# One of a step's 72 columns of samples fetched by plain DMAs from register addresses, issued by SyncE and ScalarE

## The reference

```
x = x + L0(gn(x))   3x3 convolution, then 64x64
x = x + L1(gn(x))   deformable 3x3 convolution, two groups of 32 channels
x = x + L2(gn(x))   focal modulation: depthwise 3x3, 5x5, 7x7 with gelu, gates, modulator
x = x + L3(gn(x))   triangle product of two sigmoid gates, a third gate
```

## Time and profile before

| | |
|---|---|
| median of 3 runs | 12371.41 us (12371.2 to 12372.86) |
| the profiled execution: time, span | 12375.1 us, 12373.3 us |
| granted TensorE clock, mean | 0.773 |
| busy: PE, DVE, ACT, POOL | 7826.9, 5178.4, 1654.1, 8754.7 us |
| DMA | 101 GB/s on average |

### The profile page before, as it was taken

How to read it: one execution, slowest core, us unless ns; L and a number is a source line. 1 busy time by engine, 2 the same in 40 slices (tenths; PEclk the granted TensorE clock), 3 DMA queues, 4 the chain that set the end, 5 groups by cost and what they waited for, 6 DMA issues and landing times.

```text
span 12373.3 us, 133594 instructions
## 1 busy us (share of the span) xinstructions
PE 7826.9 (63%) x46178; PEld 6378.0 (52%) x46178; DVE 5178.4 (42%) x6138; ACT 1654.1 (13%) x2837; POOL 8754.7 (71%) x9269
## 2 busy tenths in 40 slices
PE   5766667666467765554457775655457776655488
PEld 3554455545457644444447654444446664444474
DVE  3344444443344444343344444343344444344333
ACT  1011111110011112110001111210001111211015
POOL 3777777777777777777777777777777777777700
PEclk8887778877678877776678877777678887877689
DMA  2333334333244422432234422332224432343271
GB/s 86 102 88 97 111 89 111 105 94 102 73 125 160 130 66 78 115 95 61 67 102 146 167 68 71 100 110 71 57 80 146 171 93 64 92 112 91 62 248 56
DMA packets 878254, 1255.70 MB, mean 101 GB/s; under 512 B 183384, under 2 KB 663320, under 8 KB 860248
## 3 DMA queue, kind: packets, MB, share of 16 engines
q0 software_dynamic: 294912, 604.57, 19.2%
q1 hardware_dynamic: 512216, 601.04, 14.4%
q10 hardware_dynamic: 70912, 47.20, 1.2%
HBM read 1069.49 MB, written 245.50 MB: 106 GB/s over the span
## 4 chain that ended last, share of the span: by engine, by line
POOL 68%; issue 23%; PE 4%; DVE 1%; DMA 1%; ACT 0%; POOLq 0%; PEld 0%; SPq 0%; PEldq 0%; ACTq 0%; DVEq 0%
POOL gathered L471 68%; PE stage L1033 2%; PE stage L926 1%; DVE srow L1561 0%; DMA gathered<-table,idx 0%; PE acc L926 0%; DVE gathered L1554 0%; PE pt L926 0%; POOLq L469 0%; PE wtb L926 0%; PE acc L1175 0%; PEld acc L1175 0%; PE stage L988 0%; POOLq L467 0%; POOLq L477 0%
## 5 line engine op out<-in xcount | busy, mean ns | idle before, releaser
L471 POOL DMA_INDIRECT gathered<-table,idx x9216 | 8730.2, 947 | 2979.2 <-issue 2801.6
L1175 PE MATMUL acc<-stt,room 128*128 128x128 f32 (+1 forms) x30600 | 4372.0, 308 | 234.6 <-ACT stt L901 234.6
L1175 PEld LDWEIGHTS acc<-stt,room 128*128 128x128 f32 (+1 forms) x30600 | 4220.1, 221 | 543.5 <-ACT stt L901 341.5
L1164 PE MATMUL pt<-mat,srow 128*128 128x128 f32 x2048 | 507.2, 394 | 3682.6 <-DVE srow L1561 3682.2
L1164 PEld LDWEIGHTS pt<-mat,srow 128*128 128x128 f32 x2048 | 327.5, 196 | 3882.9 <-DVE srow L1561 3870.6
L1530 DVE COPY idx<-idxn 128x18 uint32<-128x18 uint32 x512 | 98.1, 192 | 5195.8 <-DMA gathered<-table,idx 5187.5
L1561 DVE TENSOR_REDUCE srow<-gathered 128x576 f32<-128x2304 f32 x512 | 2081.1, 4065 | 0.1
L1554 DVE TENSOR_TENSOR gathered<-gathered,wtb 128x2304 f32<-128x2304 f32 x512 | 1306.1, 2551 | 63.0 <-DMA gathered<-table,idx 62.6
L901 ACT ACTIVATE stt<-pt 128x512 f32<-128x512 f32 x512 | 305.9, 597 | 5968.0 <-PE pt L1164 5965.6
L926 PE MATMUL stage<-room,mat 128*128 128x512 f32 (+1 forms) x1360 | 791.4, 712 | 296.6 <-DVE room L1425 70.8
L1033 PE MATMUL stage<-room 128*128 128x128 f32 x7680 | 890.2, 278 | 12.8 <-DMA room<-toep 10.6
(11 more groups left out here) (206 smaller groups left out, 3931.7 us busy)
## 6 DMA issues: line engine op xcount, KB each, us to landing
gathered<-table,idx POOLq DMA_INDIRECT x9216
room<-toep SPq DMA_DIRECT2D x64, 1792.0 KB, 19.0
room<-toep SPq DMA_DIRECT2D x64, 1280.0 KB, 11.5
room<-toep SPq DMA_DIRECT2D x64, 768.0 KB
table<-room SPq DMA_DIRECT2D x64, 512.0 KB, 2.9
toep<-in_taps SPq DMA_DIRECT2D x128, 224.0 KB
toep<-in_taps SPq DMA_DIRECT2D x128, 160.0 KB
room<-in_x SPq DMA_DIRECT2D x4, 4096.0 KB
```

Source lines behind the costliest of these rows:

```text
L471: nc.gpsimd.indirect_dma_start(gat[r][:, k % K9 * G + k // K9, :], None, table[b].rearrange("(n e) -> n e", e=PAIR), bass.IndirectOffsetOn ...
L1164: ins = nc.tensor.transpose(pt[:, m, :], srow[r % 2][:, m * P:(m + 1) * P], M["ident"])
L1175: ins = nc.tensor.matmul(acc[a][:, 0:W], wk[0:kk, m, dx, block_at * C:block_at * C + P], stt[s][0:kk, m, dx:dx + W], start=start and m == ...
```

## The change

POOL leaves out the last column (`AT_K` = 17) of row 0 (`AT_R`) in every step but the first. For this column DVE writes the next step's addresses, the index times 64, into `column` (inside `indices`, behind L1525). At time 1 of step n, SP stores that column of 128 addresses to `column_d` in DRAM, waits until it has landed, and waits until row 0 of step n is summed. It then loads eight addresses from DRAM into registers and issues eight plain DMAs of 512 bytes, one per pixel, each from the address in a register; it does so eight times in the step, two blocks for each row, for pixels 0 to 63. ScalarE does the same for pixels 64 to 127: at time 1 it waits for `column_out` and for `summed`, and its blocks stand at 3r + 1 and 3r + 1.5, ahead of its copy L901 of the row. DVE waits for `pixels_in` ahead of row 0 of step n + 1. Two semaphores (`folded`, `moved`) go; `next_image` drains DVE instead.

```diff
+AT_R, AT_K = 0, GK - 1
+CHUNK = 8
...
+        column_d = nc.dram_tensor("column_d", [STEPS, P], I32).ap()
...
 # POOL
                     for r in range(ROWS):
                         v = n * ROWS + r
+                        own = GK if r != AT_R or isinstance(n, int) else AT_K
...
-                        for k in range(GK):
+                        for k in range(own):
...
 # SP
+                def fetch_column(n):
+                    sp.wait_ge(column_given, n)
+                    sp.dma_start(column_d[ds(n, 1), :].rearrange("o p -> p o"), column[:]).then_inc(column_out, 16)
+                    sp.wait_ge(column_out, 16 * n)
+                    sp.sem_inc(started, 1)
...
+                        if k == 0:
+                            fetch_column(n + 1)
+                            sp.wait_ge(summed, n * ROWS + AT_R + 1 + ROWS)
+                            sp.sem_inc(started, 1)
+                        per = P // CHUNK // 2 // ROWS
+                        for q in range(per * k, per * (k + 1)):
+                            yield 3 * k + 1 + 3 * (q % per) / per
+                            fetch_pixels(n + 1, nb, q)
...
 # ACT
+                def fetch_pixels(n, b, q):
+
+                    act.load(regs, column_d[ds(n, 1), CHUNK * q:CHUNK * (q + 1)])
+                    for j in range(CHUNK):
+                        at = act.snap(regs[j], min_val=0, max_val=(NPAIR - 2) * PAIR)
+                        act.dma_start(pixel(CHUNK * q + j), table[b][ds(at, ENTRY)].unsqueeze(0)).then_inc(pixels_in, 16)
...
                     for r in range(ROWS):
+                        yield 3 * r + 1
+                        if r == 0 and not last:
+                            act.wait_ge(column_out, 16 * n + 16)
+                            act.wait_ge(summed, n * ROWS + AT_R + 1 + ROWS)
+                            act.sem_inc(started, 1)
+                        per = P // CHUNK // 2 // ROWS
+                        for q in range(per * r, per * (r + 1) if not last else 0):
+                            yield 3 * r + 1 + (q % per) / per
+                            fetch_pixels(n + 1, nb, P // CHUNK // 2 + q)
                         yield 3 * r + 2
...
 # DVE
+                    if not (isinstance(n, int) and n == 0):
+                        if not (isinstance(n, int) and n == 1):
+                            dve.wait_ge(column_out, 16 * n - 16)
+                        ts(column[:], idxn[:, AT_R, AT_K:AT_K + 1], float(PAIR), None, ALU.mult).then_inc(column_given, 1)
...
-                    dve.wait_ge(landed[r], 16 * GK * (n + 1))
+                    dve.wait_ge(landed[r], 16 * GK + 16 * (AT_K if r == AT_R else GK) * n)
+                    if r == AT_R and not (isinstance(n, int) and n == 0):
+                        dve.wait_ge(pixels_in, 16 * P * n)
```

More of the change, by code:

```diff
@@ L242, in build @@
         idx = sb("idx", [P, ROWS, GK], U32)
+        column = sb("column", [P, 1], I32)
         wtn = sb("wtn", [P, ROWS, GK, 4])
@@ L371, in build @@
         table_out = sems("table_out0", "table_out1")
-        off_in, off_used, chain, idx_given, wt_given, moved, started = sems(
-            "off_in", "off_used", "chain", "idx_given", "wt_given", "moved", "started")
+        off_in, off_used, chain, idx_given, wt_given, started = sems(
+            "off_in", "off_used", "chain", "idx_given", "wt_given", "started")
+        column_given, column_out, pixels_in = sems("column_given", "column_out", "pixels_in")
         landed = sems(*(f"landed{r}" for r in range(ROWS)))
@@ L439, in planes, with pixel @@
             return d[b].rearrange("c (h r) w -> r c h w", r=2)[par, :, ds(4 * t, 4), :]
+        def pixel(p):
+            return gat[AT_R][p:p + 1, AT_K % K9 * G + AT_K // K9, :]
         def half(a, par, n=C):
@@ L474, in step @@
                                 .then_inc(landed[r], 16)
+                step(0, 0)
                 for b in range(NB):
-                    with pool.Fori(b * PER, (b + 1) * PER) as n:
+                    with pool.Fori(max(b * PER, 1), (b + 1) * PER) as n:
                         step(n, b)
@@ L671, in start @@
                     load_offsets(0, 0, 0)
+                regs = [sp.alloc_register(f"at{j}") for j in range(CHUNK)]
+                def fetch_column(n):
[4 more added lines that the diff above has]
+                def fetch_pixels(n, b, q):
+                    sp.load(regs, column_d[ds(n, 1), CHUNK * q:CHUNK * (q + 1)])
+                    for j in range(CHUNK):
+                        at = sp.snap(regs[j], min_val=0, max_val=(NPAIR - 2) * PAIR)
+                        sp.dma_start(pixel(CHUNK * q + j), table[b][ds(at, ENTRY)].unsqueeze(0)).then_inc(pixels_in, 16)
                 def step(n, b, i):
@@ L687, in step @@
                         sp.dma_start(x2[:, 2 * STEPS * W:(2 * STEPS + 1) * W], xs[:, 0, :]).then_inc(x2_out, 16)
-                    if b == 0:
-                        for k in range(ROWS):
-                            yield 3 * k + 1
+                    last = isinstance(n, int) and n == STEPS - 1
+                    for k in range(ROWS):
+                        yield 3 * k + 1
+                        if b == 0:
                             bands(ROWS * i + k)
+                        if last:
+                            continue
+                        if k == 0:
[6 more added lines that the diff above has]
+                            fetch_pixels(n + 1, nb, q)
                 meet = meeting(sp)
@@ L892, in close, with fetch_pixels @@
                         act.dma_start(out[:, ds(n(u) * TILE, TILE)], res[u]).then_inc(res_out[u], 16)
+                regs = [act.alloc_register(f"at{j}") for j in range(CHUNK)]
+                def fetch_pixels(n, b, q):
+                    act.load(regs, column_d[ds(n, 1), CHUNK * q:CHUNK * (q + 1)])
+                    for j in range(CHUNK):
+                        at = act.snap(regs[j], min_val=0, max_val=(NPAIR - 2) * PAIR)
+                        act.dma_start(pixel(CHUNK * q + j), table[b][ds(at, ENTRY)].unsqueeze(0)).then_inc(pixels_in, 16)
                 def step(n, b, i):
+                    last = isinstance(n, int) and n == STEPS - 1
+                    nb = b + 1 if isinstance(i, int) and i == PER - 1 else b
                     for r in range(ROWS):
+                        yield 3 * r + 1
[7 more added lines that the diff above has]
+                            fetch_pixels(n + 1, nb, P // CHUNK // 2 + q)
                         yield 3 * r + 2
@@ L1357, in context_fold @@
                     scale(S["wq"], M["wq"])
-                    scale(gws[:], gw[:]).then_inc(folded, 1)
+                    scale(gws[:], gw[:])
                     yield 13
@@ L1362, in context_fold @@
                     tt(b_q2, PB[2][:, 1:2], V["b_q"], ALU.add)
[L1363 removed]
+                    tt(b_gate2[0:8, :], PB[2][0:8, 2:3], b_gate, ALU.add)
                 def operands_fold(b, i):
                     yield 11
[L1367 removed]
+                    scale(S["ccen"], M["ccen"])
                     yield 13
                     dve.wait_ge(shift_p, 2 * b + 2)
[L1370 removed]
+                    nc.vector.tensor_copy(b_cen, PB[2][:, 0:1])
                 def context(b, i):
@@ L1565, in next_image @@
                 def next_image(b):
-                    nc.vector.tensor_copy(base[:], base0[:]).then_inc(moved, 1)
-                    dve.wait_ge(moved, b + 1)
+                    nc.vector.tensor_copy(base[:], base0[:])
+                    dve.drain()
                 def start():
```

5 lines of the change are left out of this document (1 added, 4 removed).

## The result

| | before | after |
|---|---|---|
| median | 12372.01 us (4 runs beside the changed kernel's) | 13202.49 us (13182.17 to 13212.49, 4 runs) |
| ratio | | 1.0669, 95% interval 1.0655 to 1.0683: slower |
| span of the profiled execution | 12373.3 us | 13208.0 us |
| gathers on POOL | 9216 | 9089 |

The direction was as forecast, the size was not: +830 us where +273 was the forecast, and above the end of the range, 12950. (On some chips the kernel before itself took 18367 to 18585 us in place of 12375; what ran there stands in one table under group 3 and is compared with nothing else.)

A forecast was written before the change was run, and what follows sets the result against it. POOL's gather queue was taken to bound the kernel. Three images losing 118 (depthwise) + 26 (modulate) make 432 us, less 159 saved: +273 on 12375.1, 12648, set at 12645 for the median; range 12205 to 12950.

The forecast's parts named there:

- POOL bounds the kernel before; 127 gathers are worth 159 us: POOL's gather queue never stands still, 1.252 us per gather; leaving out one in 127 steps saves 159 us.
- SP's eight blocks fit, DVE's operation and the wait in SP's step cost nothing: SP idles most of a step, so 41 us of blocks fit; DVE's 0.2 us and SP's first wait cost nothing.
- ScalarE's blocks stand in the chain and turn the gain into a loss: ScalarE runs in order; most blocks delay copies TensorE's products need, losing 432 us in three images against 159 gained.
- A block costs c = 5.1 us: One load of eight registers, 1.65 us, plus eight DMA issues at 0.43, 3.4 us; bounds 2.2 and 18.4.
- A depthwise step is 90.5 + 4c: From g, the last gelu's end, to the same place next step: 110.9 us against 88.9, 22 lost per step.
- Modulate is 54.5 + 8c: Step length in the stage behind depthwise, all eight blocks in the way: 95.3 us, 26 us lost over four steps.
- Operands, close and table steps: Steps of 46 to 53 + 8c, 87 to 94 us, losing few us that light steps (without background) take up.
- free lag: POOL needs row 0's sum only three rows later, so 58 us of lateness cost nothing and light steps win them back.
- Rival 1: The chain keeps up and POOL stays full: 12212 us; needs a depthwise step under 96 us; chance 0.22.
- Rival 2: The block is cheap, about 2.4 to 3.1 us; at 2.4 a depthwise step is 100.1, total 12308; chance 0.10.
- Rival 3: A block's load costs several trips to DRAM: 12933 us at c = 6.6, 14000 above 8; 0.10 with rival 4.
- Rival 4: The pixels come late for DVE at next step's row 0; decides only with c near 8; 0.10 with rival 3.

The follow-up runs named there:

- group 3: Runs with one register load per block or with pixels split 96 to 32, and repeats of other runs, on chips where the kernel before took 18366.87 to 18584.81 us.
- e1: Changed kernel with nobody fetching the left-out column: no address store, no blocks on SyncE or ScalarE; 12215.75 us, ratio 0.9871 to the kernel before.
- e2: Changed kernel with ScalarE's 64 pixels left out, SyncE storing the addresses and fetching its 64; 12217.13 us, ratio 0.9872 to the kernel before.
- e3: Changed kernel with SyncE's 64 pixels left out, SyncE only storing the addresses and ScalarE fetching its 64; 13090.23 us, ratio 1.0578 to the kernel before.
- e5b: Changed kernel with ScalarE's waits kept and its blocks taken out; 12220.06 us, ratio 0.9875 to the kernel before.
- e7b: Changed kernel with ScalarE's register loads taken out and its 64 DMAs kept, from fixed addresses; 12438.22 us, ratio 1.0049 to the kernel before.
- e4: Changed kernel with ScalarE's two blocks of a row, and the waits ahead, moved behind the row's second copy; 12992.84 us, ratio 1.0499 to the kernel before.
- e8b: Changed kernel with all 128 pixels fetched by SyncE in sixteen one-load blocks, none by ScalarE; 13841.36 us, ratio 1.1185 to the kernel before.
- e10b: Changed kernel with column_d as one fixed row, so one register load per block, not two; 20301.12 us, against 18366.87 before on the same chip.

## Why the prediction was wrong in size

By its own steps:

- **POOL bounds the kernel before; 127 gathers are worth 159 us.** Right: 158.4 (e1).
- **SP's eight blocks fit, DVE's operation and the wait in SP's step cost nothing.** Right by themselves: 1.4 us (e2). Beside ScalarE's blocks SyncE's cost 112 us (e3), most of them in image 0, and why stays open.
- **ScalarE's blocks stand in the chain and turn the gain into a loss.** Right, and shown: with them 13090 to 13202, without them 12217 to 12220.
- **A block costs c = 5.1 us.** The issues were 0.40, not 0.43: 3.2 us in place of 3.4. The load was said to be "one trip to DRAM", 1.65 us. It is two loads of 1.10 us and their register work, 2.4. So c = 5.7, and this term was mis-sized. The nearest row for the price of one load was a fair guide (1.10 for 1.65); that the source line stands for two was not seen, and no row of the kernel before could show it. By the prediction's own formula c = 5.75 gives 8 x 24.6 - 58 = 139 and 4 x 11.6 = 46 per image, 3 x 185 - 159 = +396. This explains 123 of the 557 us that are missing.
- The two prices that were quoted beside it from the Trainium skill: "Runtime: NRT & Kernel Launch", "Instruction fetch mechanics", 200 ns per register even in bulk; the rows give 1.10 us for eight, 0.14 each, and the same 1.10 for one, so by the trace it is a price per load and not per register. "DMA: Bandwidth & Descriptors", "Latency and other measured facts", 600 ns as the floor; the minimum in the trace is 0.99 (a pointer's load on SyncE), and no load came near 0.6.
- **A depthwise step is 90.5 + 4c.** The slope is about right: 4.7 and 4.2 between the kernels above. The fixed part is 93 (e5b) in place of 90.5, and the blocks under the bands add some four: 16.4 us from the gelus' end to the copy's (4144.88 to 4161.29) where 2c + 0.6 is 12.1; and a table load of 1.28 us shows behind the wait. 118 against 113.5 by the formula: 8 x 4.5 x 3 = 108 us. The blocks of row 0 begin at g + 35 (first pixel at g + 37), where 33 was the forecast, but not for its reason. SP stores the column when `indices` are done, at g + 24 and not at g + 18, and the blocks begin 10.5 us after that. A landing of 6.5 us or more belongs to any step; 2.0 were assumed, the quickest landing of a small DMA in the earlier trace rows. At most 4 of the 10.5 can be the bands' doing. (Whether the column would pass the bands on another queue was not tried. In the trace of the kernel before, a store of ScalarE's, issued on its own queue at 3828.76, landed at 3850.44, and the last band at 3850.02: that one did not pass them.)
- **Modulate is 54.5 + 8c.** 100.5 at c = 5.75, measured 99: right.
- **Operands, close and table steps lose "few us that the light steps beside them take up".** This is the step that failed: a term put at nothing. Operands are 103 us by measurement, 92 to 99 by 46 to 53 + 8c; triangle 102, and no formula was written for it; close 92. (4 x 13.7 + 2 x 13.4 + 4 x 3.4) = 95 us per image, 286 in three. And image 0 loses 75 us, where nothing was set down. The trace has the blocks in the way of the background's own operations too: in an operands step ScalarE idles on its own queue 24 us ahead of L959 and 41 ahead of L878 and L889, in all 65, where the kernel before has 0.2. The argument "the light steps take it up" is wrong in itself. A light step returns lag, so that the chain is early again (those without background take 74 us, not the 88.9 of the forecast); it does not return time in which POOL stood still. The 58 us of free lag are spent once, in the depthwise stage, and modulate, operands, triangle and close follow with only one light step between them (the norm, 83 us).
- **Together:** 123 (c) + 108 (depthwise) - 18 (modulate) + 286 + 75 = 574, against the missing 557. The terms are not exact (step lengths are means, and the free lag is nearer to 50 than to 58), so that they meet within 17 us is in part luck.
- **The rivals.** Rival 1 (the chain keeps up, 12212) asked for a depthwise step under 96 us. e5b, with no block at all, is that case: 93 us and 12220. The condition was right, and the block of 5.7 us was four times the 1.5 that rival 1 could bear. Rival 2 (c = 2.4, 12308) is near e7b, which has that block and gave 12438: 104 us where 100.1 was reckoned. Rival 3 (c = 6.6, 12933) was closest in time though c was lower: it had the stages behind modulate as small as the forecast did. Rival 4 (the pixels come late) did not decide here, 26 us of waiting; it did in e4, with the same c and the blocks elsewhere, which the prediction expected only near c = 8.
- **The range.** Its upper end followed from c up to 6.6 alone. The doubt about the stages that were reckoned in half a sentence was as large, and was not in it.

## What to carry over

A DMA issue or a register load takes no busy time, but it takes its place in the queue of an engine that runs in order; before such work is put on an engine that looks 12% busy, add up its length in the queue per loop (46 us here) and see which engines wait for what stands behind it, and who waits for what it brings (e4). A step's stages each have their own limit: write the formula for every stage, and remember that lag can be won back and standstill of the bounding engine cannot. An engine with idle time may be idle because it is one part of a loop (e8b): what has to fit is the work and the latencies of the loop together, 18 + 77 + 3 us here, not the work alone.

## What the runs showed of the hardware that was not expected

- A load of eight words from DRAM into registers takes 1.10 us (median; 1.04 at least, up to 5.3), and a load of one pointer the same (0.99 to 5.9). With SP's bands in flight ScalarE's loads take 4.0 in the median, and a pair of blocks read 13.84 us in place of 9.06. A DRAM tensor that is addressed with a loop's counter costs such a pointer load each time; a fixed address does not (e10b).
- A plain DMA of 512 bytes from a register's address is issued in 0.226 us, and with its register work one follows another in 0.40; from a fixed address in 0.30 (e7b). For comparison an indirect DMA for 128 such pixels costs POOL 1.25 us: 128 plain ones cost 70 us of a queue (e8b). The trade was 1.25 us of one engine's queue for some 46 of each of two others'.
- A column of 128 words, one from each partition, takes 6.5 us at least and 7.8 in the median from its issue to its landing in DRAM (24.9 at most, behind the bands), where the quickest of ScalarE's `gated` stores took 2.0.
